# A bank for every second turned value matrix, a fold between turns, and own rows copied ahead of the exponentials, in the first three steps of six local-attention layers

## The reference

```python
x = q                                          # (4, 512, 128)
x = layernorm(x + attn(x))                     # 16 heads of 8, ALiBi bias, softmax, Wo, bo
# local transformer, 6 layers, 16 heads of 64, window 32, tokens shifted by one
for i in range(6):
    x = attn_layer(shift_tokens(x), Wqkv[i], q_scale[i], k_scale[i], Wo[i]) + x
    x = ffn_layer(shift_tokens(x), ln_g[i], ln_b[i], W1[i], b1[i], W2[i], b2[i]) + x
x = layernorm(x1 + x)                          # x1: the input of the local transformer

def attn_layer(x, Wqkv, qs, ksc, Wo):
    q, k, v = split(x @ Wqkv)                  # heads of 64
    q, k = rotary(l2norm(q) * qs), rotary_inverse(l2norm(k) * ksc)
    sim = einsum('bhwie,bhwje->bhwij', q, k of this window and the one before) * 8
    out = softmax(mask(sim)) @ v
    return out @ Wo
def ffn_layer(x, g, bln, W1, b1, W2, b2):
    a, gate = split(layernorm(x, g, bln) @ W1 + b1)
    return a * gelu(gate) @ W2 + b2
```

## Time and profile before

| | us |
|---|---|
| median of 3 runs (lowest to highest) | 1930.24 (1928.96 to 1932.67) |
| the profiled execution | 1930.84 |
| its span in the profile | 1929.1 |
| mean granted clock of TensorE | 0.979 of full |
| TensorE matmul busy | 1792.7 |
| VectorE, ScalarE, GpSimd busy | 1532.0, 1361.0, 1279.4 |

### The profile page before, as it was taken

The page is one execution under the profiler, slowest core; times in us unless marked ns, Lnnn a source line. Parts: engine busy times, 40 slices in busy tenths (PEclk is TensorE's granted clock), DMA queues, the critical chain, the costliest instruction groups (busy, mean ns, idle before and its releaser), DMA issues.

```text
span 1929.1 us, 60125 instructions
## 1 busy us (share of the span) xinstructions
PE 1792.7 (93%) x24400; PEld 1025.2 (53%) x24400; DVE 1532.0 (79%) x2549; ACT 1361.0 (71%) x2867; POOL 1279.4 (66%) x1223
## 2 busy tenths in 40 slices
PE   6898899669999999999999999999999999999996
PEld 3443444345555555555555555555555555555553
DVE  5778787348888888888888888888888888788874
ACT  2454444447788778887788777887788877887781
POOL 4303210238888877888877887788878878788851
PEclk8999999889999999999999999999999999999998
DMA  3400000323433334333344333343333333333320
GB/s 81 97 2 28 2 2 2 88 53 73 95 81 82 82 73 95 75 73 76 81 88 96 73 68 81 81 92 83 72 85 81 90 73 67 79 82 79 68 50 22
DMA packets 138769, 132.64 MB, mean 69 GB/s; under 512 B 79352, under 2 KB 85048, under 8 KB 138168
## 3 DMA queue, kind: packets, MB, share of 16 engines
q1 hardware_dynamic: 138496, 128.81, 30.0%
HBM read 20.94 MB, written 1.05 MB: 11 GB/s over the span
## 4 chain that ended last, share of the span: by engine, by line
POOL 56%; issue 19%; PE 4%; DVE 1%; ACT 1%; POOLq 0%; DVEq 0%; ACTq 0%
POOL prob L1269 9%; POOL kfin L1297 6%; POOL kfin L1294 6%; POOL kfin L1293 6%; POOL qfin L1302 6%; POOL qfin L1301 6%; POOL sumq L1311 5%; POOL kfin L1298 4%; POOL sumk L1289 4%; POOL sumk L1290 3%; POOL lower L1307 1%; PE bank_z L893 1%; PE bank_y L901 1%; PE bank_z L1058 1%; PE bank_a L882 1%
## 5 line engine op out<-in xcount | busy, mean ns | idle before, releaser
L1097 ACT ACTIVATE prob<-s_in,lower,rq 128x64 f32<-128x64 f32 x1536 | 535.0, 431 | 0.3
L882 PE MATMUL bank_a<-x_shift,wqk_sb 128*128 128x512 f32 x768 | 365.2, 598 | 6.0 <-ACT sq L1243 4.3
L1083 ACT ACTIVATE zT<-bank_z 128x1024 f32<-128x1024 f32 x192 | 192.7, 1017 | 74.0 <-PE bank_z L893 72.5
L1269 POOL TENSOR_TENSOR prob<-prob,rden 128x1024 f32<-128x1024 f32 x96 | 182.6, 1902 | 90.5 <-DVE rden L1361 84.8
L1297 POOL TENSOR_TENSOR kfin<-rk,kfin 128x512 f32<-128x512 f32 x96 | 122.2, 1273 | 150.5 <-ACT rk L1224 95.6
L882 PEld LDWEIGHTS bank_a<-x_shift,wqk_sb 128*128 128x128 f32 x768 | 144.8, 192 | 140.4 <-issue 128.1
L396 ACT ACTIVATE a_prob<-a_sT 128x1024 f32<-128x1024 f32 x128 | 130.5, 1023 | 105.2 <-PE a_sT L221 103.0
L518 DVE TENSOR_REDUCE a_negmax<-a_max 128x1 f32<-128x512 f32 x256 | 164.6, 684 | 48.9 <-PE a_max L171 45.3
L901 PE MATMUL bank_y<-zT,wvo_low 128*128 128x512 f32 x384 | 187.2, 610 | 0.6 <-ACT zT L1083 0.4
L901 PE MATMUL bank_y<-zT,wvo_high 128*128 128x512 f32 x384 | 187.0, 610 | 0.0
L893 PE MATMUL bank_z<-pT,xk_prev 32*128 32x128 f32 x3072 | 165.1, 284 | 11.3 <-DVE xn L1394 8.0
(11 more groups left out here) (205 smaller groups left out, 4124.9 us busy)
## 6 DMA issues: line engine op xcount, KB each, us to landing
kpad<-kfin SPq DMA_DIRECT2D x384, 128.0 KB, 2.4
qpair<-qfin SPq DMA_DIRECT2D x384, 128.0 KB, 2.4
wqk_sb<-in_wqkv SPq DMA_DIRECT2D x40, 128.0 KB, 2.7
xk_prev<-xk_own SPq DMA_DIRECT2D x24, 192.0 KB, 2.4
ffn_sb<-in_ffn SPq DMA_DIRECT2D x6, 537.5 KB, 4.3
wvo_low<-in_wqkv SPq DMA_DIRECT2D x6, 256.0 KB, 4.7
wvo_low<-in_wo SPq DMA_DIRECT2D x3, 512.0 KB, 5.7
wvo_high<-in_wqkv SPq DMA_DIRECT2D x6, 256.0 KB, 5.1
```

What stands on the lines that cost most here:

```text
L882: last = pe.matmul(bank_a[:, half, :], wqk_sb[:, layer_of(u) % 2, part, half, g * P:(g + 1) * P], cols(u), start=True, stop=True)
L1083: return act.activation(out, in_, ACT.Copy)
L1097: last = act.activation(prob[:, n % 2, i, :], s_in[:, n % 2, i, :], ACT.Exp, bias=lower[:, n % 2, i:i + 1], scale=rq[:, n % 2, i:i + 1])
L1269: pool.tensor_tensor(prob[:, e % 2], prob[:, e % 2], rden[:].unsqueeze(2).broadcast_to([P, TPB * GH, 2 * WIN]), ALU.mult).then_inc(pn_ok, 1)
```

## The change

Three things, all in steps 0 to 2. Turns 1, 5 and 9 go into `bank_z[:, 0]`, so they no longer wait for the copy of the turn before; turn 9 waits instead for the masks' addition of quarter 0 (`mask_ok`), which reads that bank. ScalarE copies them right behind turns 0, 4 and 8, ahead of the exponentials and the second square. In the tail, turn 4s + 2 comes ahead of fold 4s + 1, and its copy ahead of that fold's even heads. And the own rows of sequence 0 (step 2) are copied behind these two copies, ahead of all exponentials; for the other sequences the copy stays where it was.

```diff
--- before.py
+++ after.py
@@ -810,6 +810,10 @@
 
         wvT = zT[:].rearrange("p a w t h q -> p (a w t h q)")[:, 0:2 * INNER].rearrange("p (l q c) -> p l q c", l=2, c=P)
 
+        def turned_bank(i):
+
+            return bank_z[:, 0, :] if i % 4 == 1 else bank_y[:]
+
         def raw_values(layer, p):
 
             return wvo[layer].rearrange("p h c -> p (h c)")[:, p * P:(p + 1) * P]
@@ -920,9 +924,12 @@
             def turn_values(i):
                 layer, q = divmod(i, 2)
                 after(pe, vo_loaded[layer], 0, 48)
-                after(pe, wvT_ok, i - 1)
+                if i % 4 == 1:
+                    after(pe, mask_ok, i // 4 - 2)
+                else:
+                    after(pe, wvT_ok, i - 1)
                 for k in range(PAIRS // 2):
-                    last = pe.matmul(bank_y[:, k * P:(k + 1) * P], raw_values(layer, 4 * q + k), ident[:],
+                    last = pe.matmul(turned_bank(i)[:, k * P:(k + 1) * P], raw_values(layer, 4 * q + k), ident[:],
                                      start=True, stop=True, is_transpose=True)
                 last.then_inc(vturn_mm, 1)
 
@@ -1000,8 +1007,8 @@
                     after(pe, pk_ok, n)
                     project(n, 0, q_mm)
                 if s < FOLD_STEPS:
+                    turn_values(4 * s + 2)
                     fold(4 * s + 1)
-                    turn_values(4 * s + 2)
                     turn_values(4 * s + 3)
                     fold(4 * s + 2)
                     fold(4 * s + 3)
@@ -1086,7 +1093,7 @@
                 after(act, vturn_mm, i)
                 after(act, fold_mm, 2 * (i // 2 - 1) - 1)
                 at = slice(4 * (i % 2), 4 * (i % 2) + 4)
-                copy(wvT[:, i // 2 % 2, at].rearrange("p q c -> p (q c)"), bank_y[:]).then_inc(wvT_ok, 1)
+                copy(wvT[:, i // 2 % 2, at].rearrange("p q c -> p (q c)"), turned_bank(i)).then_inc(wvT_ok, 1)
 
             def even_heads(i):
                 after(act, fold_mm, i)
@@ -1192,6 +1199,10 @@
                         act.activation(sq[:, 0, :], bank_a[:, 0, :], ACT.Square).then_inc(sqk0_ok, 1)
                     if s < FOLD_STEPS:
                         values_turned(4 * s)
+                        values_turned(4 * s + 1)
+                    if rows_at(c) == 0:
+                        act.wait_ge(xk_mm, 1)
+                        copy(xk_own[:, 0].rearrange("p t c -> p (t c)"), bank_z[:, 2, :]).then_inc(xk_ok, 1)
                     if quarter(d):
                         after(act, lower_ok, d)
                         after(act, pT_ok, d - 2)
@@ -1200,14 +1211,12 @@
                     if quarter(n):
                         after(act, pk2_ok, n)
                         act.activation(sq[:, 1, :], bank_a[:, 1, :], ACT.Square).then_inc(sqk_ok, 1)
-                    if s < FOLD_STEPS:
-                        values_turned(4 * s + 1)
                     if s == 0:
                         act.wait_ge(const_ok, 1)
                     if quarter(d):
                         exponentials(d, 3, 12)
                     u_own = rows_at(c)
-                    if u_own is not None:
+                    if u_own:
                         after(act, xk_mm, u_own)
                         after(act, z_mm, 4 * (u_own - 2) + 3)
                         copy(xk_own[:, u_own % 2].rearrange("p t c -> p (t c)"), bank_z[:, 2, :]).then_inc(xk_ok, 1)
@@ -1249,8 +1258,8 @@
                         z = zT[:, e % 2].rearrange("p w t h q -> p w (t h q)")
                         copy(z[:, 0:2, :], bank_z[:, 0:2, :]).then_inc(z01_ok, 1)
                 if s < FOLD_STEPS:
+                    values_turned(4 * s + 2)
                     even_heads(4 * s + 1)
-                    values_turned(4 * s + 2)
                     values_turned(4 * s + 3)
                     even_heads(4 * s + 2)
                     even_heads(4 * s + 3)
```

## The result

| | us |
|---|---|
| before, median of 7 runs | 1930.56 (1927.12 to 1935.51) |
| changed, median of 7 runs | 1922.38 (1916.27 to 1925.95) |
| ratio changed to before | 0.995, 95% interval 0.9933 to 0.9966 |
| the profiled execution of the changed kernel | 1924.42, its span 1922.6 |
| mean granted clock of TensorE | 0.981 of full |

The kernel is 9.7 us faster by the ratio, which is that of the means (6.6 to 12.9), and 8.2 by the medians. The forecast was 12.8 us and 1917.4, with 1914 to 1923 as the range. The ratios of the later runs leave out two executions that lie far off, one of 3462.65 us of the kernel before and one of 1951.34 of e1.

The account below looks back on a forecast made before the run. TensorE was taken to set the middle's beat, so only steps 0 to 2 could gain: 1.6 + 1.5 + 10.4 = 13.5 us, less 0.9 and plus 0.2 for the clock, giving 12.8. Median forecast 1917.4, range 1914 to 1923.

Parts of the forecast that it names:

- Steps 0 and 1: Turns and copies closer together and an earlier turn in the tail: 1.6 us from step 0, 1.5 from step 1.
- up to 1.0 more: Step 0, fold 0: packed closer, the clock may hold and win up to 1.0 us more; 0.2 was taken.
- Step 2, the copies: Step 2: three ScalarE copies in a row let fold 8 start at 409.75, 4.43 us earlier.
- The delayed square: Step 2: keys' second square about 1.0 us late, with 1.2 cover; rival that the wait passes to it, chance 0.05.
- Step 2, fold 8 to the logarithm: Step 2, fold 8 to the keys' logarithm: 5.51 us at the fast clock, as in step 1, instead of 8.63.
- Step 2, the tail: End of step 2, folds 10 and 11: 0 to 1.84 us lost to a fallen clock; 0.9 was taken.
- The first rival: Step 2: the clock falls around 410 despite the shorter gap, gain 8.0 us, time 1922.2; chance 0.12.
- main case: Whole kernel: the forecast gain comes about, with its own range of 1914.4 to 1920 us; chance 0.75.
- a gain that is lost: Later steps: a load or queue with its own time holds them back, time stays 1928 to 1932; chance 0.05.
- a slower beat: Steps 3 to 95 lock into another beat; 0.2 us more in each ends at 1935; chance 0.03.

Follow-up runs that it names:

- e1: Kernel before with only the own rows' copy moved, behind the copy of turn 8; ratio to before 0.9985, ramp (layers' start to GpSimd's third mark) 64.64 us.
- e8: The changed kernel profiled a third time, unaltered; ratio to before 0.996, ramp 62.84 us.
- e4: The changed kernel run once more, unaltered; ratio to before 0.9951, ramp 63.33 us.
- e9: Changed kernel plus one 128x512 and one 128x256 unread product ahead of fold 8 in step 2; ratio to before 0.994, ramp 61.18 us.
- e10: Changed kernel with step 2's last four exponentials behind the copy of turn 11, plus e9's filler; ratio to before 0.9933, ramp 58.26 us.
- e6: Changed kernel plus four unread 128x512 products in step 2's tail, between fold 9 and turn 11; ratio to before 0.9957, ramp 61.09 us.
- e7: Changed kernel with step 2's last four exponentials moved behind the copy of turn 11; ratio to before 0.996, ramp 60.11 us.
- e12: Kernel before plus four unread 128x512 products in the wait ahead of fold 8; ratio to before 1.0007, ramp 70.05 us.
- e11: Changed kernel with the own rows' copy back behind nine exponentials; one execution, no ratio, ramp 67.57 us.
- e3: Kernel before with only the tail reordered: turn 4s + 2 and its copy earlier; ratio to before 0.9991, ramp 69.28 us.
- e2: Kernel before with only the second bank and early copies of turns 1, 5 and 9; ratio to before 0.9994, ramp 70.22 us.

## Why the prediction was right, and what was off

**Steps 0 and 1.** Step 0, from its key projection to that of step 1, was to give 1.6 and gave 2.7 (19.69 before, 16.99 after); the surplus is fold 0 at 1.16 for 1.69 and what stands behind it, the "up to 1.0 more" of which 0.2 was taken. Step 1 was to give 1.5 and gave 1.54.

**Step 2, the copies.** Fold 8 was to start 4.40 behind step 2's key projection (409.75 against 405.35) and started 4.41 behind it (410.26 against 405.85), and 4.42 in e8. In e4 it was 6.02, since the clock had fallen at the end of step 1. The delayed square cost nothing: TensorE did not wait for GpSimd's sum in this step in any of the three profiles.

**Step 2, fold 8 to the logarithm: the term that was mis-sized.** 5.51 was taken from step 1; measured are 6.66, 6.93 and 8.08. About 1 us of it is the stop in the scores (0.87, 1.14 and 0.98). The trace of before doesn't show it, nor do the five others whose scores ran slow throughout. In the third profile the clock fell inside the scores besides. Where the clock held, the way less the stop is 5.79, 5.79, 5.78 (e9) and 5.78 (e10), so 0.3 of the difference to step 1 is something else, which stays open.

**Step 2, the tail.** I took 0.9 for the clock. From the copy of turn 10 to the end of fold 11 it took 7.54, 7.54 and 6.46 instead of 5.27, so 2.3, 2.3 and 1.2. That TensorE's empty 2 us do it is shown by all profiles together: in eleven of them TensorE is idle for 1.99 to 2.58 ahead of turn 11, and the clock fell in ten; e6 fills the gap, e7 and e10 shorten it to 1.18 and 0.79, and in all three the late folds take 1.16. The first rival, the clock falling in spite of the short gap, is real, and 0.12 looks too little for it. In e1 fold 8 itself was slow, behind 1.77 us. In the changed kernel fold 8 was fast in all three profiles, but in e8 the clock fell some 2.5 us later, inside the scores, and so it did in e6 and e7 with the same instructions up to there: three profiles out of five with this front. With e9's filler in the gap (e9, e10) it held in both, too few to say that the filler does it.

**The sum.** Predicted for the ramp 12.8; measured 11.24, 8.72 and 9.21, mean 9.7, as much as the ratio says (9.7, 9.5 and 7.7 us in the three comparisons, each known to 3 or 4 us). The median, 1922.38, lies in the range, but outside the main case's own 1914.4 to 1920 and beside the 1922.2 of the first rival. It isn't that rival's sum that came true, which had fold 8 and everything behind it slow: what is missing is the stop, the 0.3 beside it, and a clock that fell in the tail in all three profiles and once each at the end of step 1 and in the scores; step 0 gave part of it back. That the range took this in is partly luck, since it was widened for another case. Nor are runs of one kernel 3.7 us apart, as taken from three of them: the seven here spread over 8.4. That the gain carries through to the end is right to about 2 us: from the third mark to the last it took 1420.3 to 1422.4 in the changed kernel, 1420.4 and 1420.7 before. The rivals of a gain that is lost and of a slower beat are out.

**What stays open.** Why the clock in step 0 fell in three profiles out of five with the same code ahead of it. And why the four kernels with fillers (e6, e9, e10, e12), and e11, needed 1424.2 to 1426.7 from the third mark to the last: e6 and e12 have eleven stops of TensorE behind the ramp where the others have six to eight, but one profile each doesn't tell whether that is the reason.

## What to carry to other kernels

Where TensorE's clock falls behind a wait, price the slow stretch with the wait: in step 2 the own rows' wait was 4.7 us and is now 1.7, and the way from step 2's first projection to the keys' logarithm is shorter by 17.46 - 11.07 = 6.4. But then also look at the idle pieces that are left, for the clock can fall there: here behind 1.7 us in some executions, and behind 2 us in most. A single profile doesn't tell which, so take two or three. Compare traces by distances inside a stage; here the part ahead of the layers differed by up to 10 us between executions of the same instructions, more than the effect.

## What the runs showed of the hardware that I had not expected

**Stops of TensorE at fixed places of its program.** Six times behind the ramp in the kernel before, seven in the first profile of the changed one, TensorE stands for 0.5 to 1.4 us, released by nothing in the profile. The one in step 2's scores and the one at six products from the end (1644.88) are at the same product in all three profiles of the changed kernel, and e6 and e9 moved them by exactly the instructions that were added, by eight and by four products. Counted from the start of the program they didn't move. The one in step 2's scores stands behind 2769 matmuls in all seven profiles that show it in the timeline, with and without the fillers, and two others stand in all fourteen profiles of all kernels: one behind 10904 or 10905 matmuls (0.67 to 1.38 us), one behind 20907 or 20908 (0.62 to 1.04). Of the other places each execution shows some, six to eleven stops of 0.5 us or more in all, and the length varies too. That TensorE is short of instructions there is only argued: the profile shows no transfer for them.

**The part ahead of the layers.** It ended between 361.85 and 371.83 us in fourteen profiles, with the same instructions. A spread of 10 us there is of the size of the spread of the whole time (1916 to 1926 in seven runs of the changed kernel), and single parts, worth 2 to 7 us in the ramp, could not be told from none by the whole time (e1 to e3).

**The clock's fall is a matter of the execution as much as of the gap.** Behind a wait of 1.77 us fold 8 was slow in e1. Behind one of 1.65 or 1.66 the clock held in the changed kernel's first profile and fell 2 to 3 us after the wait's end, inside the scores, in e8, e6 and e7. And with the same 1.99 us of waiting the tail of step 2 kept it in e1 and lost it in e2.
